# A triangular solve split into 16-step blocks, and filters as Toeplitz products through DRAM, in a two-layer decoder kernel

## What is computed

```python
A = jnp.einsum('bhncd,bhned->bhnce', kbc, kc)
T = eye + jnp.tril(A, -1)
inv = jax.scipy.linalg.solve_triangular(T, jnp.broadcast_to(eye, T.shape), lower=True, unit_diagonal=True)
u = inv @ vc
w = inv @ kbc
# a scan over the 4 chunks gives delta_out, with a state of 32 x 32 a head
paths = [_fir(v_direct, f) for f in (fir_w3, fir_w7, fir_w15, fir_w31)] + [delta_out]
router_in = jnp.concatenate([hidden_states] + [p.reshape(B, L, H * DV) for p in paths], axis=-1)
ctx = sum((probs[..., i:i + 1] * paths[i] for i in range(5)))
```

## Time and profile before

| | |
|---|---|
| median of 3 runs | 1015.66 us (1011.92 to 1016.79) |
| the profiled execution's own time | 1015.0 us |
| its span, first to last instruction | 1013.2 us |
| mean granted TensorE clock | 0.958 |
| busy: PE / DVE / ACT / POOL | 940.2 / 731.4 / 653.3 / 334.9 us |
| the four filters, PE L921 | 106.4 us |
| the solve, DVE L1583 + L1588 | 61.2 + 61.4 us |
| DMA queue q1 | 77584 packets, 44.04 MB |

### The profile page before, as it was taken

How to read it: one execution, slowest core, us unless ns; L and a number is a source line. 1 busy time by engine, 2 the same in 40 slices (tenths; PEclk the granted TensorE clock), 3 DMA queues, 4 the chain that set the end, 5 groups by cost and what they waited for, 6 DMA issues and landing times.

```text
span 1013.2 us, 22026 instructions
## 1 busy us (share of the span) xinstructions
PE 940.2 (93%) x7958; PEld 601.1 (59%) x7958; DVE 731.4 (72%) x2866; ACT 653.3 (64%) x1531; POOL 334.9 (33%) x720
## 2 busy tenths in 40 slices
PE   7988999999995879999999999999977889999996
PEld 4777675645432546668776756565334555777675
DVE  2565769899998876857563688777899996764624
ACT  4498989886553235677987778566543246778743
POOL 3766323633322011537322422141240022433222
PEclk9799999999997699999999999999986999999998
DMA  9400000121353221100000000103543210000001
GB/s 314 164 1 1 1 2 11 43 53 43 95 121 65 58 54 32 43 11 22 1 13 1 1 12 22 45 9 84 115 106 74 62 36 11 11 12 1 11 1 32
DMA packets 77692, 45.44 MB, mean 45 GB/s; under 512 B 53008, under 2 KB 68880, under 8 KB 77328
## 3 DMA queue, kind: packets, MB, share of 16 engines
q1 hardware_dynamic: 77584, 44.04, 16.5%
HBM read 33.01 MB, written 11.01 MB: 43 GB/s over the span
## 4 chain that ended last, share of the span: by engine, by line
PE 69%; DVE 16%; ACT 7%; DMA 2%; POOL 2%; issue 2%; SPq 1%; ACTq 0%; POOLq 0%; DVEq 0%
PE psum L1102 7%; PE psum L995 7%; PE psum L921 6%; PE psum L559 6%; PE psum L1092 3%; PE psum L860 3%; PE psum L832 3%; PE psum L834 3%; DVE pool L1583 3%; PE psum L1086 3%; PE psum L1088 3%; DVE sol_t L1588 3%; PE psum L568 2%; ACT pool L1818 2%; ACT pool L2023 2%
## 5 line engine op out<-in xcount | busy, mean ns | idle before, releaser
L1804 ACT ACTIVATE pool<-psum 128x512 f32<-128x512 f32 x144 | 83.3, 596 | 58.1 <-PE psum L921 27.9
L1818 ACT ACTIVATE pool<-pool,small 128x128 f32<-128x128 f32 x224 | 91.6, 484 | 38.3 <-POOL small L2185 38.1
L559 PE MATMUL psum<-sb_const,pool 128*128 128x128 f32 x672 | 99.1, 282 | 9.6 <-ACT pool L1818 2.8
L921 PE MATMUL psum<-pool,firw 128*32 128x512 f32 (+7 forms) x960 | 106.4, 578 | 0.1
L2180 POOL TENSOR_SCALAR small<-small 128x4 f32<-128x4 f32 x88 | 22.2, 252 | 249.9 <-DVE small L1174 247.8
L559 PEld LDWEIGHTS psum<-sb_const,pool 128*128 128x128 f32 x672 | 78.3, 145 | 38.3 <-issue 19.0
L2183 POOL TENSOR_TENSOR small<-small,minus_half 128x4 f32<-128x4 f32 x88 | 92.3, 1049 | 7.3
L995 PE MATMUL psum<-pool,sb_l1a 128*128 128x512 f32 x192 | 92.1, 632 | 2.1 <-ACT pool L1804 2.1
L1102 PEld LDWEIGHTS psum<-sb_l1f,pool 128*128 128x128 f32 x640 | 78.3, 192 | 15.6 <-issue 13.9
L1102 PE MATMUL psum<-sb_l1f,pool 128*128 128x128 f32 x640 | 83.5, 278 | 0.0
L1405 DVE TENSOR_TENSOR pool<-pool,psum 128x512 f32<-128x512 f32 x80 | 52.7, 681 | 38.7 <-ACT pool L2090 16.6
(11 more groups left out here) (428 smaller groups left out, 2146.4 us busy)
## 6 DMA issues: line engine op xcount, KB each, us to landing
pool<-scratch_kk SPq DMA_DIRECT2D x18, 256.0 KB, 3.7
pool<-in_cF SPq DMA_DIRECT2D x16, 256.0 KB, 3.3
scratch_kk<-pool SPq DMA_DIRECT2D x10, 256.0 KB, 2.6
pool<-in_xF SPq DMA_DIRECT2D x8, 256.0 KB, 6.1
pool<-in_x SPq DMA_DIRECT2D x8, 256.0 KB, 6.2
scratch_xt<-pool SPq DMA_DIRECT2D x8, 256.0 KB, 2.0
pool<-scratch_xt SPq DMA_DIRECT2D x8, 256.0 KB, 3.2
...
```

Source lines behind the costliest of these rows:

```text
L559: m = e.transpose(f.ap[:, part(b)], src[:, part(b)], ident)
L921: m = e.matmul(b4(f.ap)[32 * c:32 * c + 32, :, 4 * kg:], firw[:, col, :], vsh[:, c, :, 0:P - 4 * kg], start=n == 0, stop=n == len(kgs) - 1)
L1804: e.activation(slot(g, i), f.ap, ACT.Copy).then_inc(f.emptied, 1)
L1818: m = e.activation(dst[:, part(b)], src[:, part(b)], ACT.Identity, bias=v["nm"][:, b:b + 1], scale=v["r"][:, b:b + 1])
```

## The change

**Filters.** One tile `toeplitz` (128 x 64 x 64) holds for each channel the taps of all four filters as a 46 x 64 matrix: 46 input tokens (16 plus 30 of history) by 16 outputs of each of four filters. It is built once by the new SP step s_t, by way of DRAM: two DMAs of zeros, 64 of single taps, 46 of two rows each. b_sh now waits for b_vT, stores v (slot 2) to a zero-padded scratch in two DMAs, and loads it back as windows in eight DMAs: 46 rows (tokens) x 8 blocks of 16 tokens x 64 channels, at partitions 0 to 45 and 64 to 109. PE's b_fir is 2 parts of 64 matmuls, one for a channel pair's half each: 46 rows, 32 outputs (blocks), 64 columns (16 tokens x 4 filters). ACT evacuates four tiles of 128 x 512; the new SP steps b_fs store them in 64 B pieces (4 DMAs, 4096 pieces each) and b_fl loads them as channels on partitions into slots 3 to 6 (4 DMAs). b_r and b_mx wait for these loads. b_ez and `firw` go.

**Solve.** Each 32 x 32 matrix is inverted as two diagonal blocks of 16: b_x is now 30 instructions of (k + 1)(15 - k) elements, k = 0 to 14. POOL's b_sol lays the unit rows, its b_rs a copy of the later unit rows. The block between comes from PE: b_i1 (four transposes), b_i2 (64 small matmuls in four banks; ACT evacuates with scale -1), b_i3 (64 small matmuls, one evacuation); b_u waits for it. The inverse is in slot 12 now, the right-hand sides in slot 13.

**Loading.** Weights are loaded in pieces: four used once go to an arena tile, `unit_rows` is not loaded, `ones` is kept as one column. DRAM scratch gets three new arrays.

**Walk.** The list is a new one; s_t stands behind c_nb/0, b_vT/g and b_sh/g earlier, right behind b_v/g and b_vs/g for most groups.

```diff
--- before.py
+++ after.py
...
+CB = CH // 2
...
+TB, NBLK = 16, P // 16
+NLAG = TB + max(FIRS) - 1
...
-f_d.0-2/0 c_fa/1 c_na/2 c_pT/3 f_d.3/0 x_ex/7 x_pT/6 c_hF/2 f_e.5/0 f_d.4/0 c_pv/3 f_d.5/0 c_nb/1 x_v/7 f_tr/1 c_na/3
-f_out/0 x_pv/6 f_lg/1 x_pT/7 f_na/0 f_lt/1 c_hF/3 x_pv/7 f_mu/1 x_na/6 f_hid.0-1/1 b_tr/0 x_hF/6 b_q/0 x_na/7 b_v/0
...
+b_ks/0 b_vs/0 c_v/6 b_k2/0 f_e.0-2/1 b_vT/0 c_fa/2 f_hid.3-5/1 c_ex/6 f_d.0-1/1 b_sh/0 c_nb/2 c_ft/3 f_d.2/1 f_e.3/1
+b_ss/0 f_e.4-5/1 c_pT/6 c_ex/7 f_d.3-5/1 f_out/1 c_pv/6 b_qn/0 c_fa/3 c_pT/7 c_v/7 b_gg/0 f_tr/2 f_na/1 f_lg/2
+b_fir.0-1/0 c_na/6 b_fs.0/0 f_lt/2 f_mu/2 b_tr/1 f_hid.0-1/2 c_pv/7 c_hF/6 c_nb/3 c_w1/6 b_k/1 b_v/1 f_tr/3 f_lg/3
+c_na/7 b_kk/0 f_cnt/2 c_ft/6 b_ag/0 f_lt/3 c_hF/7 c_w1/7 f_gl/2 c_fa/6 c_ft/7 f_hid.2/2 f_gw/2 f_e.0-1/2 b_vs/1 b_vT/1
...
+b_qs/1 b_q2/1 b_fir.0-1/1 b_fs.0/1 f_na/2 f_cnt/3 c_park/6 b_fs.1/1 b_x.16-17/0 f_hid.0-1/3 f_gl/3 b_x.18-21/0 b_tr/2
...
+    toeplitz, itau = sb("toeplitz", [P, HALF, HALF]), sb("inverse_tau", [P, NH])
+    lags = nc.dram_tensor("scratch_taps", (P, 4 * HALF), F32, kind="Internal").ap()
+    padded = nc.dram_tensor("scratch_v", (NG, 2, GB, P + CH, HALF), F32, kind="Internal").ap()
+    paths = nc.dram_tensor("scratch_fir", (NG, 4, CH, P, TB), F32, kind="Internal").ap()
...
+    def windows(g):
+        return slot(g, 8, 4).rearrange("p (n c) -> p n c", c=HALF)
+    MOVED = {"v": 2, "windows": 10, "sums": 14, "paths": 18}
...
+    def blocks(g):
+        both = slot(g, 12, 2)
+        return both[:, 0:3 * CB * CB].rearrange("p (m i) -> p m i", i=3 * CB), both[:, 3 * CB * CB:].rearrange("p (j i) -> p j i", i=CB)
...
+        def s_t(g, k):
+            o.wait_ge(sem("zeros_laid"), 1)
+            zeros = flat(toeplitz[:, 0:CH, :])
+            e.dma_start(lags, zeros[:, 0:4 * HALF]).then_inc(sem("toeplitz_laid"), 16)
+            e.dma_start(padded.rearrange("g r b t c -> (g r b) (t c)")[:, 0:CH * HALF], zeros[0:NG * 2 * GB]).then_inc(
+                sem("toeplitz_laid"), 16)
+            o.wait_ge(sem("toeplitz_laid"), 32)
+            first = cols["once_l1"]["fir"][0]
+            for f, k in enumerate(FIRS):
+                kg, n = FIR_GROUPS.index((f, 0)), (k + 3) // 4
+                for s, c in itertools.product(range(4), range(4)):
+                    at = HALF * f + TB - 1
+                    src = dram["once_l1"][CH * s:CH * s + CH, first + 4 * kg:first + 4 * (kg + n)].rearrange("p (k c) -> c p k", c=4)
+                    dst = lags[CH * c:CH * c + CH, at:at + 4 * n].rearrange("p (k s) -> s p k", s=4)
+                    e.dma_start(dst[s], src[c], allow_slow_non_contiguous=True).then_inc(sem("toeplitz_laid"), 16)
+            o.wait_ge(sem("toeplitz_laid"), 32 + 16 * 16 * len(FIRS))
+            by_half = lags.rearrange("(r c) (f z) -> r (c f) z", r=2, z=HALF)
+            blocks_ = toeplitz.rearrange("p c (f t) -> p (c f) t", t=TB)
+            for lag in range(NLAG):
+                lo = NLAG - 1 - lag
+                e.dma_start(blocks_[lag:P:HALF], by_half[:, :, lo:lo + TB]).then_inc(sem("toeplitz_laid"), 16)
         def b_sh(g, k):
-            a = g % NA
-            vsh = slot(g, 8, 4).rearrange("p (c m) -> p c m", c=4)
-            kept = dram["xt"][g].rearrange("q (h m) -> (q h) m", h=2)
-            o.wait_ge(sem("v_made"), g + 1)
+            f = fill("b_vT", g)
+            o.wait_ge(f.emptied, f.n)
             upper_half(o, g)
-            e.dma_start(kept, slot(g, 5)).then_inc(sem(f"v_out{a}"), 16)
-            o.wait_ge(sem(f"v_out{a}"), 16 * (g // NA + 1))
-            for s in range(4):
-                e.dma_start(vsh[32 * s:32 * s + 32, :, s:],
-                            kept.rearrange("(c p) m -> p c m", c=4)[:, :, 0:GT - s]).then_inc(sem(f"shifted{a}"), 16)
+            for r in range(2):
+                e.dma_start(padded[g, r, :, CH:, :].rearrange("b t c -> t b c"),
+                            b4(slot(g, 2))[:, :, HALF * r:HALF * r + HALF]).then_inc(*path(g))
+            moved(o, g, "v")
+            for r, b in itertools.product(range(2), range(GB)):
+                at = padded[g, r, b, CH + TB - NLAG:CH + TB - NLAG + 1]
+                src = bass.AP(padded.tensor, at.offset, [[HALF, NLAG], [TB * HALF, NBLK], [1, HALF]])
+                e.dma_start(windows(g)[HALF * r:HALF * r + NLAG, NBLK * b:NBLK * b + NBLK], src).then_inc(*path(g))
+        def b_fs(g, k):
+            for r in range(2):
+                f = fill("b_fir", g, f"r{r}", k)
+                o.wait_ge(f.emptied, f.n)
+                dst = paths[g, 2 * r + k].rearrange("n p t -> p n t")
+                e.dma_start(dst, slot(g, 3 + 2 * r + k).rearrange("p (n t) -> p n t", t=TB)).then_inc(*path(g))
+        def b_fl(g, k):
+            moved(o, g, "sums")
+            by_channel = paths[g].rearrange("r (u f) (j n) t -> j (r u) f (n t)", f=4, j=4)
+            for j in range(4):
+                e.dma_start(slot(g, 3, 4)[j:P:4].rearrange("p (f m) -> p f m", f=4), by_channel[j]).then_inc(*path(g))
...
+            for d in range(2):
+                d_ = slice(CB * d, CB * d + CB)
+                src = dram["kk"][g].rearrange("r (j i) -> r j i", i=CH)[:, d_, d_]
+                e.dma_start(blocks(g)[1][HALF * d:HALF * d + HALF], src).then_inc(*chunks(g))
...
-            o.wait_ge(made, MADE["s_b2"])
-            o.wait_ge(sem("edge_zeroed"), 3 * g + 3)
-            o.wait_ge(sem(f"shifted{g % NA}"), 64 * (g // NA + 1))
-            f = begin("b_fir", g, "s", k)
-            vsh = slot(g, 8, 4).rearrange("p (c b t) -> p c b t", c=4, b=GB)
-            kgs = [kg for ff, kg in FIR_GROUPS if ff == k]
-            for n, kg in enumerate(kgs):
-                for c in range(4):
-                    col = FIR_GROUPS.index((k, kg)) * 4 + c
-                    m = e.matmul(b4(f.ap)[32 * c:32 * c + 32, :, 4 * kg:], firw[:, col, :],
-                                 vsh[:, c, :, 0:P - 4 * kg], start=n == 0, stop=n == len(kgs) - 1)
-            m.then_inc(f.filled, 1)
+            o.wait_ge(sem("toeplitz_laid"), 32 + 16 * 16 * len(FIRS) + 16 * NLAG)
+            moved(o, g, "windows")
+            halves = [begin("b_fir", g, f"r{r}", k) for r in range(2)]
+            for u, j, r in itertools.product(range(8), range(4), range(2)):
+                c, r_, j_ = CH * k + 4 * u + j, slice(HALF * r, HALF * r + NLAG), slice(CH * j, CH * j + CH)
+                m = e.matmul(halves[r].ap[j_, HALF * u:HALF * u + HALF], windows(g)[r_, :, c], toeplitz[r_, c, :],
+                             start=True, stop=True)
+                if u == 7 and j == 3:
+                    m.then_inc(halves[r].filled, 1)
...
+        def b_i1(g, k):
+            chunked(o, g, "turned")
+            turn(begin("b_i1", g), slot(g, 12))
+        def b_i2(g, k):
+            got("b_i1", g)
+            kkt = slot(g, 8, 4).rearrange("p (q t) -> p q t", q=NP)
+            for c in range(4):
+                f, r_ = begin("b_i2", g, f"c{c}"), slice(CH * c, CH * c + CB)
+                for b in range(GB):
+                    for h in range(NH):
+                        m = e.matmul(f.ap[CH * h:CH * h + CH, CB * b:CB * b + CB], kkt[r_, h * GB + b, CH * c:CH * c + CH],
+                                     small[g]["turned"][r_, b * NH + h, :], start=True, stop=True)
+                m.then_inc(f.filled, 1)
+        def b_i3(g, k):
+            for c in range(4):
+                got("b_i2", g, f"c{c}")
+            o.wait_ge(sem("unit_beside"), g + 1)
+            f = begin("b_i3", g)
+            for n in range(NP):
+                for h in range(NH):
+                    h_ = slice(CH * h, CH * h + CH)
+                    m = e.matmul(f.ap[h_, CB * n:CB * n + CB], hd(slot(g, 14))[h_, n, :], by_chunk_row(g)[h_, n, CB:],
+                                 start=True, stop=True)
+            m.then_inc(f.filled, 1)
...
-            chunked(o, g, "turned")
+            got("b_i3", g)
...
-            got("b_fir", g, "s", 3)
+            moved(o, g, "paths")
...
+            x, a = blocks(g)
+            x = x[:, :, CB:2 * CB]
             k, second = divmod(k, 2)
-            nm, ni = k // 2 + 1, CH - 1 - k
+            nm, ni = k + 1, CB - 1 - k
...
-            evacuate("b_fir", g, 3 + k, k)
+            for r in range(2):
+                f = full("b_fir", g, f"r{r}", k)
+                e.activation(slot(g, 3 + 2 * r + k), f.ap, ACT.Copy).then_inc(f.emptied, 1)
...
-        def b_ez(g, k):
-            vsh = slot(g, 8, 4).rearrange("p (c b t) -> p c b t", c=4, b=GB)
-            o.wait_ge(sem(f"shifted{g % NA}"), 64 * (g // NA + 1))
-            for s in range(1, 4):
-                settle()
-                e.memset(vsh[32 * s:32 * s + 32, :, :, 0:s], 0.0).then_inc(*mark("edge_zeroed", 3 * g + s))
+        def s_t(g, k):
+            settle()
+            e.memset(flat(toeplitz[:, 0:CH, :]), 0.0).then_inc(*mark("zeros_laid", 1))
...
+        def b_sol(g, k):
+            rows = blocks(g)[0]
+            f = fill("b_qn", g)
+            settle()
```

(12 more changed lines are left out.)

305 lines of the change are left out of this document (169 added, 136 removed).

## The result

The changed kernel takes 1245.9 us (median of 4 runs, 1242.5 to 1259.2) against 1013.8 us beside it: 1.231 times as long, with an interval of 1.221 to 1.241. The forecast was 1076 us with a range to 1118: slower, as foreseen, but by 232 us where 60 were forecast.

A forecast was written before the change was run, and what follows sets the result against it. In-order PE was taken to bound the kernel: 892 us of work, 29 of start and end idle and 156 of stalls make 1077, less 3 a span of 1074, plus 1.8 gives 1076 us; range 949 to 1118.

The forecast's parts named there:

- wait in front of b_fir/0: PE's stall before group 0's filters, behind the s_t build and then the windows: 33 us.
- the seven waits for windows: PE's stalls before b_fir in groups 1 to 7, window loads outlasting the covering PE work: 123 us.
- PE busy: TensorE's work: 940 less 106 for old filters, plus 27 new filters and 31 block between: 892 us.
- all other idle of PE: Idle at start and end, 29 us, less 3 for DVE work that lengthens the real cover.
- A: Rival: 46-row window loads run on two DMA engines and stall PE; 1076 us, own range 1022 to 1116; chance 0.64.
- L: Wait from b_vT's evacuation until the windows land: 28 us over two engines, about 10 over 16.
- The clock I cost at nothing more: PE's granted clock around the eight stalls: no extra cost, since 892 us already holds the old middle's slow places.
- The sign given for this case: In the profile after: if the small matmuls take over 35 ns each, PE's sum is the cause.
- Row and rule on the small matmuls: On PE: 24 ns a matmul by trace; the skill's 25 ns an instruction would add some 50 us; the row decides.
- The idle of the middle places: PE's 43 us idle at 200 to 400 and 720 to 840: most goes, 15 kept as waits, falling into stalls.
- B: Rival: window loads run on 16 DMA engines and are nearly covered; 946 us, faster; chance 0.25 together with D.
- D: Rival: small 64 B stores jam the DMA rings; up to 40 us in B (986), hidden in A's stalls; 0.25 with B.

The follow-up runs named there:

- z0: Changed kernel with s_t moved behind s_a, and 47 rows a window instead of 46: 1343.3 us.
- e1: Changed kernel with 48 rows a window instead of 46, nothing else: 1143.3 us (1.130).
- e4: Changed kernel with 48-row windows, s_t behind s_a, and the Toeplitz tile built by 48 DRAM-to-DRAM DMAs of 256 pieces, then two loads: 1041.5 us.
- x2: Changed kernel with the filters of before, no s_t, b_fs or b_fl; new solve and new walk stay: 1064.0 us (1.050).
- x5: Solve part alone on the walk of before: old filters, 16-step blocks, b_i1 to b_i3 between b_rl and b_u.0; one execution: 1073.3 us.
- y1: e4 with b_fs storing 128 rows of 2 KB instead of 64 B pieces, sums in another order: 1036.9 us (1.024).
- y2: Filter part alone on the walk of before, loads repaired as in e4, b_fs storing 2 KB rows, sums in another order: 1053.4 us (1.029).

## Why the prediction was wrong, point by point

The sum was 1074 us of span; 1242.8 came. The difference of 169 is made up so:

| term | forecast | measured | difference |
|---|---|---|---|
| wait in front of b_fir/0 | 33 | 116.0 | +83 |
| the seven waits for windows | 123 | 98.9 | -24 |
| PE busy | 892 | 925.7 | +34 |
| all other idle of PE | 26 | 102.2 | +76 |

Read again, the text has one slip of its own: b_fir/0 at 192 and windows at 228 make a wait of 36, not 33, so its span should have been 1077.

**The mechanism of A was right.** The loads of 46 rows ran on two engines (z0, e1), L was 25.0 us for group 1 (349.38 to 374.42) where 28 was forecast, which is most of the 24 us less in the table, and the ranking of the waits by cover held: longest for groups 7 and 3 with the least cover, shortest for 6 and for 4 with the most. A piece took 12 to 15 ns, where 15 and 2 us of landing were forecast. That SP is held while it issues was not in the text; it cost nothing of its own, for with 48 rows (e1) PE's idle in front of all other lines is the same, 94.2 us against 93.9.

**The step that failed most is s_t.** I started it at 105 (116.7), gave its 66 first DMAs 31 us, by SP's 0.43 us an issue, and they took 4.6 + 51.6 + 18.4 = 75: pieces of 4 bytes, 0.8 us an issue. I gave the 46 two-row DMAs 65 us, by the 11 ns a piece of the earlier trace rows, and they took 93 to issue, 15.7 ns a piece, before b_sh/0 could be issued. Each was priced by the best row there was and none had a range, though no row had the shape. The late start and the two prices, 12, 44 and 28 us, put b_sh/0 at 283.9 instead of 201; its windows took 26.5 us, as forecast (27), and b_fir/0 came 2 us later by itself. On one chain with no cover left these are the 83, with the slip of 3.

**PE's 34 us** are 9 on the filters (35.9 for 27), 5 on the block between (35.7 with the transposes, for 31), and 20 on matmuls that the change does not touch. The mean granted clock of the span was 0.840 instead of 0.958. "The clock I cost at nothing more" was the wrong step: behind six of the eight stalls PE works at 0.50 to 0.55. The filters show its price: 64 of their matmuls took 2.25 us at 0.50 in the changed kernel (35 ns each, group 2 above) and 1.93 at 1.00 in e4 (30 ns); the row of 24 ns had been at 1.00 too, so that shape and clock both were missing. The sign given for this case, over 35 ns a matmul, was just met (35.9 us for 1024).

**Row and rule on the small matmuls.** I took 24 to 27 ns a matmul by the earlier trace rows, some 52 us for both kinds. In e4 they were busy 61.4 us, with 18.3 of "issue" in front of their lines: 80. The row was a burst of 16 matmuls, the change has bursts of 64 and 128; it was the row of a shape, not of a length. The Trainium skill (TensorE: Matmul & The Clock Gate, Back-to-back issue gap) gives about 25 ns an instruction. By that figure both kinds together would be 102 us, an estimate; the measured 80 lie between row and rule.

**The idle of the middle places stayed.** I let 28 of 43 us go for DVE's relief, and the rest of the waits fall into the stalls. PE's waits for ACT were 39.4 us (33.6 before), for DVE 15.8 (17.9), and "issue" outside the first wait 28.6 (3.8). x2 and x5 show it without any stall: idle 82 and 87 us against 73. That three round trips and small matmuls, in part at half clock, take the place of what DVE no longer does is argued from these waits; it was not tested by itself.

**The rivals.** B, 16 engines, was given 946 us. e1 to e4 are that case: 1041.5 with the build out of the way. So B's price was 95 us too low, by the same PE, clock and idle terms, and it had no term for s_t at all: with the build as it came and only the windows on 16 engines (e1) the time is 1143.3. With B true the forecast would have been "faster" and wrong in its sign. A's right sign rests on its stalls alone: without them its terms make 918 us, "faster" too, where e4 measured 1041.5. D, the jam of the 64 B stores, is some 5 us in the new walk (y1) and 40 in the old (y2).
